# Forming the low parts of h from PSUM with one scaled operation

## The reference

```python
mod = (silu(c) @ wmod).reshape(16, 6, 1, 256)           # sa, ca, ga, sb, cb, gb
ga, gb = sign(ga) * max(|ga|, 0.25), sign(gb) * max(|gb|, 0.25)
h = layernorm(x) * (1 + ca) + sa
# attention, 8 heads of 64, over a key/value latent of 64 columns
q = h @ Wq.T;  kv = h @ Wkv_down.T;  k = kv @ Wk_up.T;  v = kv @ Wv_up.T
x = x + ga * (softmax(q @ k.T / 8) @ v) @ Wo.T
h = layernorm(x) * (1 + cb) + sb
x = x + gb * (h @ weight.T + h.reshape(.., 4, 64).sum(-2) @ disha)
```

## Time and profile before

| | us |
|---|---|
| median of 3 runs | 3259.14 |
| lowest and highest run | 3256.48, 3263.53 |
| the profiled execution | 3262.56 |
| its span | 3260.8 |
| TensorE busy | 3175.0 |
| GpSimd busy | 2584.8 |
| VectorE busy | 2200.4 |
| ScalarE busy | 1705.1 |

### The profile page before, as it was taken

The page is one execution under the profiler, slowest core; times in us unless marked ns, Lnnn a source line. Parts: engine busy times, 40 slices in busy tenths (PEclk is TensorE's granted clock), DMA queues, the critical chain, the costliest instruction groups (busy, mean ns, idle before and its releaser), DMA issues.

```text
span 3260.8 us, 44881 instructions
## 1 busy us (share of the span) xinstructions
PE 3175.0 (97%) x15398; PEld 1927.1 (59%) x15398; DVE 2200.4 (67%) x2542; ACT 1705.1 (52%) x3203; POOL 2584.8 (79%) x1513
## 2 busy tenths in 40 slices
PE   5999999999999999999999999999999999999995
PEld 3555656566566665665666565665656656666554
DVE  4657676776767767677776767767677776766652
ACT  1555555555555555555555555555555555555451
POOL 1778788887888878788887878878788887877882
PEclk7999999999999999999999999999999999999995
DMA  2111111111112011121111112111110111111111
GB/s 68 40 44 55 46 66 33 49 60 47 56 47 66 31 58 53 47 66 33 53 56 47 56 47 66 35 55 52 47 66 34 53 56 46 56 46 53 43 34 36
DMA packets 161746, 163.16 MB, mean 50 GB/s; under 512 B 58480, under 2 KB 109808, under 8 KB 161520
## 3 DMA queue, kind: packets, MB, share of 16 engines
q1 hardware_dynamic: 161520, 160.30, 15.0%
HBM read 74.66 MB, written 17.33 MB: 28 GB/s over the span
## 4 chain that ended last, share of the span: by engine, by line
PE 92%; DVE 5%; POOL 1%; issue 1%; ACT 1%; DMA 1%; SPq 0%; POOLq 0%; ACTq 0%; DVEq 0%
PE ps_mix L547 27%; PE ps_score L565 16%; PE ps_max L586 14%; PE ps_score L567 14%; PE ps_side L535 6%; PE ps_side L646 6%; PE ps_side L664 3%; PE ps_side L633 2%; DVE neg_max L984 1%; DVE w_out_lo L993 1%; POOL prob_sum L842 1%; PE ps_side L604 1%; DVE query L1027 1%; PE ps_side L653 1%; DVE h_lo L1017 1%
## 5 line engine op out<-in xcount | busy, mean ns | idle before, releaser
L842 POOL TENSOR_TENSOR prob_sum<-prob_sum,probs 128x1024 f32<-128x1024 f32 x768 | 1881.0, 2449 | 243.4 <-ACT probs L722 188.2
L984 DVE TENSOR_REDUCE neg_max<-ps_max 128x1 f32<-128x1024 f32 x1024 | 1247.9, 1220 | 755.3 <-PE ps_max L586 749.3
L722 ACT ACTIVATE probs<-ps_score 128x512 f32<-128x512 f32 x2048 | 1113.3, 598 | 969.0 <-PE ps_score L567 956.5
L547 PE MATMUL ps_mix<-probs,values 128*64 128x512 f32 x4096 | 991.6, 605 | 0.0
L565 PE MATMUL ps_score<-query,key_hi 128*128 128x512 f32 x2048 | 873.7, 427 | 1.1 <-ACT probs L722 1.1
L567 PE MATMUL ps_score<-query_m,key_lo 128*128 128x512 f32 x2048 | 805.0, 393 | 0.0
L586 PE MATMUL ps_max<-key_hi,query 128*128 128x512 f32 x2048 | 644.5, 396 | 8.3 <-DVE neg_max L984 5.4
L565 PEld LDWEIGHTS ps_score<-query,key_hi 128*128 128x128 f32 x2048 | 384.6, 188 | 326.7 <-issue 246.2
L547 PEld LDWEIGHTS ps_mix<-probs,values 128*64 128x64 f32 x4096 | 248.4, 136 | 477.8 <-issue 477.1
L842 POOL TENSOR_TENSOR prob_sum<-probs 128x1024 f32<-128x1024 f32 x128 | 328.9, 2570 | 228.6 <-ACT probs L722 228.3
L586 PEld LDWEIGHTS ps_max<-key_hi,query 128*128 128x128 f32 x2048 | 386.2, 189 | 102.3 <-DVE neg_max L984 10.9
(11 more groups left out here) (119 smaller groups left out, 2907.5 us busy)
## 6 DMA issues: line engine op xcount, KB each, us to landing
query_m<-query SPq DMA_DIRECT2D x128, 512.0 KB, 3.2
recip<-recip_scratch SPq DMA_DIRECT2D x256, 128.0 KB, 2.9
x_in<-in_L_attn_x_dram SPq DMA_DIRECT2D x32, 512.0 KB, 4.0
x_mid<-in_L_attn_x_dram SPq DMA_DIRECT2D x64, 256.0 KB, 4.5
out_dram<-x_mid SPq DMA_DIRECT2D x64, 256.0 KB, 2.2
denoms<-recip SPq DMA_DIRECT2D x512, 1.0 KB, 1.7
gates<-gates_scratch SPq DMA_DIRECT2D x16, 256.0 KB, 4.1
query_m<-max_row SPq DMA_DIRECT2D x128, 4.0 KB
```

The source lines that it names most:

```text
L547: last = nc.tensor.matmul(ps_mix[j * R:j * R + R, :], values[par][:, k, :], probs[:, s % RING, j * HALF:(j + 1) * HALF], start=(k == 0), s ...
L722: nc.scalar.activation(probs[:, s % RING, half * HALF:(half + 1) * HALF], ps_score[half], ACT.Exp, scale=SCALE).then_inc(exps_done, 1)
L842: nc.gpsimd.tensor_tensor(out=total[:, :], in0=before, in1=probs[:, s % RING, :], op=ALU.add).then_inc(adds_done, 1)
L984: nc.vector.tensor_reduce(neg_max[:, m:m + 1], ps_max[m % 2][:, :], AX_X, ALU.max, negate=True).then_inc(maxima_done, 1)
```

## The change

For `norm_t` ScalarE reads the bank once, into `h_hi`. It waits for its own result and then leaves shift minus `h_hi` in SBUF (`h_rest`), reading `h_hi`. VectorE reads the bank itself: `h_lo` = bank x scale + `h_rest`, one scalar_tensor_tensor operation. That operation, not ScalarE's, now adds to `side_drained`, and it is done in the same step's loop over side jobs, behind the rest of the step's work on VectorE, no longer a step later. For `norm2_t` the same, in two halves of 128x256: two reads into `h2_hi`, a wait, two `h2_rest` with a wait ahead of each, then two scaled operations on VectorE, the second of which frees the bank. The jobs `h2_split` are gone. `latent` and `ffn` wait for `side_drained` in place of `h_split` and `h2_split`.

```diff
@@ PE, latent
-                        need(pe, h_split, 2 * NF * b + NF * (i + 1))
+                        need(pe, side_drained, z.through("norm_t", NF * i + 1) + 1)
@@ PE, ffn
-                        need(pe, h2_split, CHUNKS * b + i + 1)
+                        need(pe, side_drained, z.through("norm2_t", i) + 1)
@@ ScalarE
-            def split_h2(z, g):
-                need(act, side_drained, z.through("norm2_t", g) + 1)
-                need(act, side_full, z.through("ffn", g - 1) + 1 if g else z.before())
-                nc.scalar.activation(h2_hi[:, :, :], h2_t[:, :, :], ACT.Copy).then_inc(h2_hi_done, 1)
...
-                    for g in range(CHUNKS):
-                        if z.has_o and z.has_c and s == z.step("h2_split", g):
-                            split_h2(z, g)
@@ ScalarE, norm_t
-                            need(act, h_split, 2 * NF * b + i - 1)
+                            need(act, side_drained, z.through("norm_t", i - 2) + 1 if i > 1 else 0)
                             cols = slice(half * HALF, (half + 1) * HALF)
-                            for part, done in ((h_hi[:, f, cols], h_hi_done), (h_whole[:, i % 2, :], side_drained)):
-                                nc.scalar.activation(part, ps_side[:, :], ACT.Identity,
-                                                     scale=mod1[:, f:f + 1], bias=mod1[:, NF + f:NF + f + 1]).then_inc(done, 1)
+                            shift = mod1[:, NF + f:NF + f + 1]
+                            nc.scalar.activation(h_hi[:, f, cols], ps_side[:, :], ACT.Identity,
+                                                 scale=mod1[:, f:f + 1], bias=shift).then_inc(h_hi_done, 1)
+                            need_alone(act, h_hi_done, 2 * (2 * NF * b + i) + 1)
+                            nc.scalar.activation(h_rest[:, i % 2, :], h_hi[:, f, cols].bitcast(F32), ACT.Identity,
+                                                 scale=-1.0, bias=shift).then_inc(h_hi_done, 1)
@@ ScalarE, norm2_t
+                            need(act, side_full, z.through("ffn", i - 1) + 1 if i else z.before())
                             for f in range(NF):
-                                last = nc.scalar.activation(h2_t[:, f, :], ps_side[:, f * CT * P:(f + 1) * CT * P], ACT.Identity,
-                                                            scale=mod2[:, f:f + 1], bias=mod2[:, NF + f:NF + f + 1])
-                            last.then_inc(side_drained, 1)
-                            if not z.has_c:
-                                split_h2(z, i)
+                                nc.scalar.activation(h2_hi[:, f, :], ps_side[:, f * CT * P:(f + 1) * CT * P], ACT.Identity,
+                                                     scale=mod2[:, f:f + 1], bias=mod2[:, NF + f:NF + f + 1]).then_inc(h2_hi_done, 1)
+                            for f in range(NF):
+                                need_alone(act, h2_hi_done, 2 * NF * (CHUNKS * b + i) + NF + f)
+                                nc.scalar.activation(h2_rest[:, f, :], h2_hi[:, f, :].bitcast(F32), ACT.Identity,
+                                                     scale=-1.0, bias=mod2[:, NF + f:NF + f + 1]).then_inc(h2_hi_done, 1)
@@ VectorE
-                    for kind, i, b, w in z.at(s - 1):
-                        if kind == "norm_t":
-                            need(dve, h_hi_done, 2 * NF * b + i + 1)
-                            need(dve, side_drained, z.through(kind, i) + 1)
-                            half, f = divmod(i, NF)
-                            cols = slice(half * HALF, (half + 1) * HALF)
-                            nc.vector.tensor_tensor(h_lo[:, f, cols], h_whole[:, i % 2, :], h_hi[:, f, cols].bitcast(F32),
-                                                    ALU.subtract).then_inc(h_split, 1)
...
-                    for g in range(CHUNKS):
-                        if z.has_o and s == z.step("h2_split", g):
-                            need(dve, h2_hi_done, CHUNKS * z.o + g + 1)
-                            nc.vector.tensor_tensor(h2_lo[:, :, :], h2_t[:, :, :], h2_hi[:, :, :].bitcast(F32),
-                                                    ALU.subtract).then_inc(h2_split, 1)
                     for kind, i, b, w in z.at(s):
...
+                        elif kind == "norm_t":
+                            need(dve, h_hi_done, 2 * (2 * NF * b + i + 1))
+                            half, f = divmod(i, NF)
+                            cols = slice(half * HALF, (half + 1) * HALF)
+                            nc.vector.scalar_tensor_tensor(h_lo[:, f, cols], ps_side[:, :], mod1[:, f:f + 1], h_rest[:, i % 2, :],
+                                                           ALU.mult, ALU.add).then_inc(side_drained, 1)
+                        elif kind == "norm2_t":
+                            need(dve, h2_hi_done, 2 * NF * (CHUNKS * b + i + 1))
+                            for f in range(NF):
+                                last = nc.vector.scalar_tensor_tensor(h2_lo[:, f, :], ps_side[:, f * CT * P:(f + 1) * CT * P],
+                                                                      mod2[:, f:f + 1], h2_rest[:, f, :], ALU.mult, ALU.add)
+                            last.then_inc(side_drained, 1)
```

More of the change, by code:

```diff
@@ L84 @@
     "norm2_t": (24, 34, 48, 56),
-    "h2_split": (25, 35, 49, 57),
     "ffn": (28, 38, 52, 62),
@@ L106 @@
     "norm2_t": (12, 14, 17, 19),
-    "h2_split": (13, 15, 17, 19),
     "ffn": (13, 16, 18, 20),
@@ L240, in adaln_block @@
         h_lo = sb("h_lo", [P, NF, T], F32R)
-        h_whole = sb("h_whole", [P, 2, HALF])
+        h_rest = sb("h_rest", [P, 2, HALF])
         latent_t = x_in[:, 0:NT // 2, :].rearrange("p t d -> p (t d)")
@@ L267, in adaln_block @@
         gates = sb("gates", [P, 2, D])
-        h2_t = sb("h2_t", [P, NF, CT * P])
+        h2_rest = sb("h2_rest", [P, NF, CT * P])
         h2_hi = sb("h2_hi", [P, NF, CT * P], F32R)
@@ L339, in adaln_block @@
         h_hi_done = sem("h_hi_done")
-        h_split = sem("h_split")
         w_hi_done = sem("w_hi_done")
@@ L349, in adaln_block @@
         h2_hi_done = sem("h2_hi_done")
-        h2_split = sem("h2_split")
         query_hi_done = sem("query_hi_done")
```

## The result

The changed kernel takes 3345.73 us (median of 4 runs, 3339.87 to 3346.09), the kernel before 3261.34 us on the same occasions: ratio 1.0256, 95% interval 1.0239 to 1.0274 (the intervals below are of the same kind). It is 84 us slower; 72 us and 3331 us were forecast, with a range of 3290 to 3385.

What follows compares the result with a forecast made beforehand. TensorE's instruction stream bounds the kernel, with 5.4 us of steady waits to give back. Stalls at the side bank in the steady slots, ramp-up and tail sum to 72 us: 3331 us, 2.2% slower, range 3290 to 3385.

Steps and rivals of the forecast that it cites:

- The bound: Steady part: TensorE's own stream bounds the kernel; relief of other engines can give back only 5.4 us.
- The first rival: Steady part: VectorE's relief decides, so the kernel is not slower, 3262 us; chance 0.08, 0.03 of it faster.
- The bank's hold: ps_side, from ScalarE's start until free: 2.44 us for norm_t (before 1.5), 3.28 for norm2_t (before 1.1).
- The third: Scaled operation competes with GpSimd for SBUF: 1.0 us more in each of eight places, 3429 us; chance 0.05.
- the fourth rival: Scaled operation is slower by itself, at half rate: 0.53 us more a place, 3387 us; chance 0.07.
- VectorE's queue: Work ahead of the scaled operations on VectorE stalls TensorE: 2.0 us after step 56, 1.3 after step 10.
- The second rival: Stretched VectorE operations shift with GpSimd's phase, queue terms shrink to 0.3 us each: 3297 us; chance 0.14.
- step 18: norm_t there: mixed_lo of step 17 moves back and meets GpSimd's addition; stall 0.1 to 0.4 us, taken 0.3.
- The steady sum: 13 slots with all the stalls, 4.5 us per slot: 58 us.
- Slot 15: Slot of batch 15, norm2_t alone: 0.7 + 0.3 + 0.3 + 2.0 = 3.3 us.
- The chain term: Ramp-up, four norm_t in a chain: waits between transposes grow from 1.63 to 2.48 us, 3.4 us in all.
- The tail: ScalarE's start to the ffn grows from 2.46 to 3.28 us, three times: 2.5; bank wanted once after 1.16: 2.1.

Runs made afterwards that it cites:

- e5: The kernel before with one number changed: the last low part of h2 made at step 60 instead of 57; 3257.46 us, ratio 0.9981.
- e4: The kernel before with its two subtractions for the low parts of h cut to 8 columns; 3252.32 us, ratio 0.9966.
- e3: The changed kernel with VectorE's scaled operations moved ahead of w_ffn_lo, w_out_lo and mixed_lo, in slots with attention; 3282.19 us, ratio 1.0065.
- e11: The changed kernel with only w_out_lo moved behind the step's side jobs on VectorE; 3300.06 us, ratio 1.0115.
- e6: e3 plus three edits: one ScalarE wait per norm2_t, mixed_hi from step 24 to 23, mixed_lo from 17 to 18; 3261.02 us, ratio 0.9996.

## Why the prediction was right

It was right in direction, in size (72 of 84 us) and in nearly every place.

**The bound.** TensorE's steady stream had 5.4 us of waits to give back and little more. e5 shows it: one number in the table gives 6.4 us, and no wait longer than 0.3 us is left. e4 gains as much, with the small relief that it is. The first rival (relief wins) falls with it, and by the changed kernel itself, which has 81 us less of VectorE's work and is slower.

**The bank's hold.** 3.28 us for `norm2_t` was 3.27 at step 24. That it is so near is in part luck, as these terms show: h_rest 0.72 and 0.51 us, measured 0.722 and 0.508; the wait of ScalarE on its own result 0.15, measured about 0.09 (1555.49 + 1.02 to 1556.60); the scaled operation 0.69 and 0.42, measured 0.744 and 0.477. Two waits came out 0.06 us shorter each, two scaled operations 0.06 longer each, and these errors cancel. The third and the fourth rival needed a stretched or a slow scaled operation: it costs 0.05 us more than the plain form, which is neither. The handover of some 0.05 us has no row of its own in the prediction; here 0.03 us pass from ScalarE's end to VectorE's start (1557.71 to 1557.74) and 0.14 from VectorE's end to TensorE's start (1558.62 to 1558.76).

**VectorE's queue.** That w_out_lo and mixed_lo stand ahead, and not ScalarE's longer chain, makes the two large losses was the central step. e3 and e11 show it: with the order changed they are gone. The second rival had these stretches shift out of the way with GpSimd's phase; w_out_lo kept its 2.85 us, mixed_lo went from 3.07 to 2.79. At step 18 the forecast had mixed_lo of step 17 meet GpSimd's addition after it moved back; its 2.70 us in place of 1.22, and the 0.23 us at step 19, gone in e6 where mixed_lo moved, bear that out.

**What was off.** The steady sum was 58, measured 69.8, of which the lower clock in step 58 is about 15; without it 55. That term was missing: the prediction priced nothing for TensorE's clock, and the trace before, whose steady waits are 0.4 us long and leave the clock at 1.00, had no row for it. The other errors partly cancel: without the lower clock some 68 us (83 - 15) stand against the 72 forecast. Slot 15 was put at 3.3 us, with 2.0 at step 57; measured 1.6 and 0.07. With no maximum left there in front of it, w_out_lo starts before the transposes (3242.18 against 3242.91 us) and is over before ScalarE's part. Step 49 of that slot loses 0.57 us, 0.3 forecast; why is not taken apart. The ramp-up was put at 3.4 us, measured 6.4. The chain term was sound: each of the three waits between transposes grew by 0.93 us, 0.85 forecast (the one of the earlier trace rows from 1.63 to 2.56). But the transposes start 1.5 us later in this execution, which kernels with the old ramp-up show too (e5: 1.5). Over all the profiles the six kernels with the new ramp-up reach the first score product 4.1 us later on average than the seven with the old one. The tail was put at 4.6 us, measured 3.1, and between e11 and e3, with the same tail, it differs by 5 us, so that neither can be called wrong.

## What to carry to other kernels

A buffer that several engines hand on in order is priced by how long each user holds it, not by how much work the users do: take the time at which the next user comes from the trace, and add up what must be over by then, with all that stands ahead in the releasing engine's own queue. An operation that frees a contended buffer goes to the front of its engine's step. And before an engine is relieved, ask what the bounding engine waits for now: here 5.4 us, and one number in the step table got them. Nor is an engine relieved by making an operation short if what makes it long is a wait for another engine.

## What the runs showed of the hardware that was not expected

TensorE's clock fell to its lower level for about 3.4 us after a stop of 2 us in a stream that was otherwise full (1.4 us after TensorE had started again, in the slot shown), and each such fall made its slot 1.5 us longer (5.7 against 4.2 us): another two thirds of the stop itself. It followed 1 of 13 stops of 1.97 us, 2 of 13 of 2.25, 5 of 13 of 2.73, and in two executions of the whole change 10 of 13 of 2.2 us; never one of 1.15 us.

Cutting the two subtractions with both inputs in SBUF from 512 columns to 8 (e4) took their means from 1678 and 1761 ns to 1190 and 1231 only, with a maximum of 2372 ns against a minimum of 156. With the subtractions gone, another operation of that kind, mixed_lo, was stretched more: its mean went from 1902 to 2504 ns.
